# A masked attention layer and its routing, moved from their own stages into the slot timetable of the self-attention

## What is computed

```
x = x + _L1_attn_ref(_layernorm(x), ...)                  # 16 heads, rope, 100 keys
x = x + _L1_xattn_ref(_layernorm(x), ctx, ctx, mask, ...) # 16 heads, 361 keys
x = x + _L1_ffn_ref(_layernorm(x), ...)                   # top 1 of 8 experts
```

```
scores = jnp.where(attn_mask[:, None, :, :], -jnp.inf, scores)
A = jax.nn.softmax(scores, axis=-1)
...
gate_logits = jnp.einsum('bsd,ed->bse', x, gate_w) + gate_b + expert_bias
top_idx = jnp.argmax(gate_logits, axis=-1)
```

## Time and profile before

| | us |
|---|---|
| median of 3 runs | 1853.81 (1851.31 to 1858.56) |
| profiled execution, its own time | 1856.58 |
| span of that execution | 1854.9 |
| PE busy in it | 1511.9 (82%) |
| DVE, ACT, POOL busy | 835.1, 668.0, 460.0 |
| mean granted clock of PE | 0.909 |

### The profile page before, as it was taken

One profiled execution on the slowest core, in us unless ns is written; L12 is line 12 of the kernel. 1 busy time (PEld: TensorE's weight loads), 2 busy tenths in 40 slices (PEclk: granted clock), 3 DMA queues, 4 the chain that ended last, 5 costly groups with the idle time before them and its releaser, 6 DMA issues. The chain is left out here.

```text
span 1854.9 us, 31750 instructions
## 1 busy us (share of the span) xinstructions
PE 1511.9 (82%) x11682; PEld 1136.9 (61%) x11682; DVE 835.1 (45%) x2354; ACT 668.0 (36%) x1339; POOL 460.0 (25%) x426
## 2 busy tenths in 40 slices
PE   4988994588888899999999938988499999419992
PEld 2555652266655566888888825655266666319991
DVE  4666445467666442122222145665367776421111
ACT  1443341456544411222222224556355555102230
POOL 1212010001223353566666410111011110130003
PEclk9999997699988899999999967999599999659996
DMA  6432333777765223777777535553777774219994
GB/s 241 135 114 81 106 112 98 160 133 128 119 103 96 57 55 87 206 192 195 204 191 199 121 86 109 108 125 95 123 134 133 132 130 83 97 54 356 342 343 123
DMA packets 262658, 264.60 MB, mean 143 GB/s; under 512 B 118012, under 2 KB 235988, under 8 KB 256916
## 3 DMA queue, kind: packets, MB, share of 16 engines
q1 hardware_dynamic: 218516, 232.01, 48.7%
q0 software_dynamic: 41152, 28.50, 8.2%
q10 hardware_dynamic: 2880, 2.62, 0.4%
HBM read 202.35 MB, written 60.48 MB: 142 GB/s over the span
## 5 line engine op out<-in xcount | busy, mean ns | idle before, releaser
L2675 PE MATMUL cross_ps_score<-cross_q,cross_k 128*128 128x250 f32 x1024 | 223.4, 376 | 0.8 <-DVE cross_q L3090 0.8
L2675 PEld LDWEIGHTS cross_ps_score<-cross_q,cross_k 128*128 128x128 f32 x1024 | 195.5, 191 | 23.8 <-DVE cross_q L3090 1.0
L3099 DVE TENSOR_TENSOR cross_prob<-cross_act_,cross_ps_score 128x250 f32<-128x250 f32 x128 | 53.2, 416 | 268.2 <-ACT cross_act_ L2795 268.2
L3178 POOL DMA_INDIRECT x_sum<-cross_ye,cross_token x64 | 128.6, 2009 | 80.7 <-ACT cross_ye L2801 68.6
L1454 DVE CUSTOM_DVE_ANT_0 attn_masked_score<-attn_ps_score,attn_mask 100x361 bf16<-100x361 f32 x256 | 123.6, 532 | 54.2 <-PE attn_ps_score L1272 46.1
L1424 ACT ACTIVATE attn_prob<-attn_ps_prob 128x400 f32<-128x400 f32 (+1 forms) x192 | 94.7, 503 | 116.0 <-PE attn_ps_prob L1314 115.1
L2822 DVE TENSOR_REDUCE cross_nmax<-cross_ps_score 100x2 f32<-100x722 f32 x128 | 112.0, 904 | 50.5 <-PE cross_ps_score L2442 46.3
L2705 ACT ACTIVATE cross_prob<-cross_ps_prob 128x400 f32<-128x400 f32 (+1 forms) x192 | 94.7, 505 | 78.5 <-PE cross_ps_prob L2476 69.1
L2687 PE MATMUL cross_ps_prob<-cross_val,cross_prob 128*125 128x256 f32 x512 | 115.8, 379 | 0.0
L2795 ACT ACTIVATE cross_act_<-cross_ps_score 128x250 f32<-128x250 f32 x128 | 48.5, 379 | 167.7 <-PE cross_ps_score L2675 167.7
L2687 PEld LDWEIGHTS cross_ps_prob<-cross_val,cross_prob 128*125 128x125 f32 x512 | 93.5, 188 | 12.8
(11 more groups left out here) (383 smaller groups left out, 2900.4 us busy)
## 6 DMA issues: line engine op xcount, KB each, us to landing
experts_w<-in_w SPq DMA_DIRECT2D x40, 1024.0 KB, 7.4
k_stack<-mixer_part SPq DMA_DIRECT2D x32, 541.5 KB, 3.6
cross_k<-in_wg SPq DMA_DIRECT2D x32, 512.0 KB
cross_k<-in_wu SPq DMA_DIRECT2D x32, 512.0 KB
cross_val<-in_wd SPq DMA_DIRECT2D x32, 512.0 KB
cross_k<-k_stack SPq DMA_DIRECT2D x32, 270.8 KB
attn_k<-k_stack SPq DMA_DIRECT2D x32, 270.8 KB
mixer_ctx<-in_ctx_t POOLq DMA_DIRECT2D x16, 361.0 KB, 4.5
```

The costliest lines, as they stand in the source:

```text
L2675: ins = nc.tensor.matmul(ps_pre[m][:, side, 0:CAP], w[s][:, k, m * P:(m + 1) * P], xt[s][:, k, :], start=(k == 0), stop=(k == KD - 1))
L3178: g.indirect_dma_start(prog.x_sum, bass.IndirectOffsetOnAxis(token[:, 2 * e + t:2 * e + t + 1], 0), ye[s][:, t, :], None, compute_op=ALU.a ...
```

## The change

`stage_self`, `stage_attention` and `stage_route1` are gone; `stage_layer1` does the work of all three up to the scatters. Its first part is the timetable of `stage_self` with the same slots. In the change:

- The slots go on for the masked layer, 12 for a sequence, written out for all 16 sequences with no hardware loop. Its head, that is the loads, the score units and the values of sequence 0, stands at slots 64 to 75, where the self-attention finishes its sequence 15 (slots 64 to 67) and the last four sequences' queries are made (slots 71 to 78).
- The rows stay in `prog.x2`; the stores and loads of rows between the stages are gone, also in `stage_combine1`. The normalised rows of the routing are kept in `prog.kept`.
- Key tiles `m_k` lie in the memory of the self-attention's query and key stacks, context tiles in that of `xt`, so that their first loads wait for the last units of sequence 15. The queries `m_q` have tiles of their own.
- The maxima of both halves go through one transpose (slot 10), behind all 8 score units, in place of two. ACT, no longer DVE, copies the values and the turned rows out of PSUM. The value bias is put through the output projection once and is part of `m_bias_sum`.
- For each sequence b of the masked layer the routing's steps run two sequences behind: moments and root at slots 7 and 8 of the period in which its projection is done, `normalise5` at 10, `turn5` at 11 on PE, the copy of the turned rows (`xt5`) on ACT at slot 0 and `gate_logits` on PE at slot 1 of the next period, `gate_biased` on DVE at slot 2. `m_to_rows`, at slot 3, waits for it, since both write `ps_misc`. The top expert is found for a group of four sequences at once, at slots 4, 6, 8 and 9. The counting follows after the last slot, as before.
- Masks have three buffers. The first two are loaded on SP's queue right behind the four loads of x, the zeroing DMA of `expert_in` (2.6 MB) behind them, and POOL turns the two masks ahead of its first root.

```diff
@@ -275,6 +275,8 @@
         self.up2 = nc.alloc_sbuf_tensor("up2", [P, NUP, GT], F32)
         at = START["w_mlp1"][0]
         self.x2 = self.packed[0:T, at:at + B * D].rearrange("t (b d) -> t b d", b=B)
+        at = START["x0_wq"][0]
+        self.kept = self.packed[0:T, at:at + B * D].rearrange("t (b d) -> t b d", b=B)
         at = START["chunk_keep"][0]
         self.act2 = self.packed[:, at:at + NUP * GT].rearrange("p (u t) -> p u t", u=NUP)
 
-def stage_attention(prog, layer):
...
-def stage_self(prog):
+def stage_layer1(prog):
...
-    SLOTS = range(STATS_AT, GROUP * (NG - 1) + STORE_4_AT + 1)
...
+    M_UNITS = NQ * NKT
+    M_FROM = NQ * B + M_UNITS
...
+    M_SCORE_AT = {0: 0, 1: 1, 2: 2, 4: 3, 5: 4, 6: 5, 7: 6, 8: 7}
...
+    M_SHIFT_B, M_LAST_AV, M_LOGITS, M_BIASED, M_ROWS, M_TURN, M_OUT = 0, 1, 1, 2, 3, 5, 7
...
+    SLOTS = range(STATS_AT, M_FROM + M_UNITS * (B + 2))
...
+    def masked_slot(slot):
+
+        return divmod(slot - M_FROM, M_UNITS) if slot >= M_FROM - M_UNITS else (None, None)
...
-                def store_x(m):
-                    sp.wait_ge(v_out, G * (m + 1))
-                    sp.dma_start(group_rows(prog.x[4], m), prog.x2[:, m * G:(m + 1) * G]).then_inc(x_stored, 16)
+                def load_half(b, h):
+                    s = b % 2
+                    if h == 0:
+                        sp.wait_ge(stored[2], KD * len(Q_PARTS) * 16 * (b // G + 1))
...
                 for m in range(NG):
                     sp.dma_start(prog.x2[:, m * G:(m + 1) * G], group_rows(prog.x[3], m)).then_inc(x_in[m], 16)
+                for b in range(2):
+                    load_mask(b)
+                sp.wait_ge(zero_set, 1)
+                sp.dma_start(prog.expert_in.rearrange("(p n) d -> p n d", p=P),
+                             zeros[:].unsqueeze(1).broadcast_to([P, TILES1 * E1_ROWS // P, D])).then_inc(zeroed, 16)
...
-                        store_x(group_at(slot, STORE_4_AT))
                         store_parts("q4", group_at(slot, STORE_4_AT))
-                sp.wait_ge(stored[2], NG * KD * len(Q_PARTS) * 16)
-                sp.wait_ge(x_stored, NG * 16)
+                    if slot == M_FROM - M_UNITS:
+                        sp.wait_ge(pe_prob, NQ * B)
+                        for h in range(2):
+                            load_half(0, h)
+                        sp.wait_ge(pe_val, B)
+                        load_src(0)
+                        for h in range(2):
+                            load_half(1, h)
+                        load_src(1)
+                    b, k = masked_slot(slot)
+                    if in_range(b) and b + 2 < B:
+                        if k == 0:
+                            load_mask(b + 2)
+                            sp.wait_ge(m_pe_val, NKT * (b + 1))
+                            load_src(b + 2)
+                        if k == M_UNITS // 2:
+                            sp.wait_ge(m_pe_prob, M_UNITS * b + M_UNITS // 2)
+                            load_half(b + 2, 0)
+                        if k == M_UNITS - 1:
+                            sp.wait_ge(m_pe_prob, M_UNITS * (b + 1))
+                            load_half(b + 2, 1)
 
...
+                def m_to_rows(b):
+                    pe.wait_ge(m_acc, b + 1)
+                    if b == 0:
+                        pe.wait_ge(m_bias, 1)
+                    if b > 0:
+                        pe.wait_ge(v_gate_bias, b)
...
+                def turn5(b):
+                    pe.wait_ge(v_norm5, b + 1)
+                    for k in range(KD):
+                        ins = nc.tensor.transpose(ps_misc[:, k * T:(k + 1) * T], prog.kept[:, b, k * P:(k + 1) * P],
+                                                  ident[0:T, 0:T])
+                    ins.then_inc(pe_turn5, 1)
+
+                def gate_logits(b):
+                    pe.wait_ge(a_xt5, b + 1)
+                    for k in range(KD):
+                        ins = nc.tensor.matmul(ps_misc[0:T, LOGIT_COLS:LOGIT_COLS + E1], xt5[:, k, :],
+                                               prog.w("f1_gate_w", KD)[:, k, :], start=(k == 0), stop=(k == KD - 1))
...
+                    b, k = masked_slot(slot)
+                    if in_range(b):
+                        m_prob_unit(b, k)
+                    if b is None:
+                        continue
+                    if in_range(b - 1) and k == M_LAST_AV:
+                        m_weigh_values(b - 1, NQ - 1)
+                    if in_range(b - 2) and k == M_LOGITS:
+                        gate_logits(b - 2)
+                    if in_range(b) and k in M_AV_AT:
+                        m_weigh_values(b, M_AV_AT[k])
+                    if in_range(b - 1):
+                        if k == M_ROWS:
+                            m_to_rows(b - 1)
+                        if k == M_TURN:
+                            m_turn_rows(b - 1)
+                        if k == M_OUT:
+                            m_project(b - 1)
+                    if in_range(b + 1):
+                        if k in M_SCORE_AT:
+                            m_score_unit(b + 1, M_SCORE_AT[k])
+                        if k == M_SHIFT:
+                            m_shift_rows(b + 1)
+                        if k == M_VALUES:
+                            m_values(b + 1)
+                    if in_range(b - 1) and k == M_TURN5:
+                        turn5(b - 1)
...
+                        m_exp(b, k)
+                        if k == M_SHIFT_B:
+                            m_shift_half(b, 1)
+                            m_values(b, NKT - 1)
+                    if in_range(b - 2) and k == M_SHIFT_B:
+                        turn5(b - 2)
+                    if in_range(b - 1):
+                        if k == M_LAST_AV:
+                            m_keep_acc(b - 1)
+                        if k == M_TURN:
+                            m_turn_rows(b - 1)
+                    if b == -1 and k in (0, 6):
+                        m_select_heads(k // 6)
+                    if in_range(b + 1):
+                        if k == M_SHIFT:
+                            m_shift_half(b + 1, 0)
+                        if k == M_VALUES:
+                            for t in range(NKT - 1):
+                                m_values(b + 1, t)
...
+                def m_project(b):
+                    ve.wait_ge(m_base, b + 1)
+                    ve.wait_ge(m_pe_out, b + 1)
+                    nc.vector.tensor_tensor(prog.x2[:, b, :], ps_misc[0:T, 0:D], base[b % 2][:], ALU.add).then_inc(m_out, 1)
+                    ve.wait_ge(m_out, b + 1)
+                    nc.vector.bn_stats(stats4[:, b % 2, :], prog.x2[:, b, :]).then_inc(v_stats5, 1)
+
...
+                    if in_range(b - 2) and k == M_BIASED:
+                        gate_biased(b - 2)
+                    if in_range(b - 1):
+                        if k == M_ROWS:
+                            m_to_rows(b - 1)
+                        if k == M_OUT:
+                            m_project(b - 1)
+                    if in_range(b + 1) and k in M_SCORE_AT:
+                        m_score_unit(b + 1, M_SCORE_AT[k])
+                        if M_SCORE_AT[k] == M_NU - 1:
+                            m_split_shift(b + 1)
+                    if in_range(b - 1):
+                        if k == M_MEAN:
+                            means5(b - 1)
+                        if k == M_NORMAL:
+                            normalise5(b - 1)
+                    if in_range(b - 2) and (b - 2) % G == G - 1 and k in M_ROUTE_AT:
+                        route((b - 2) // G, M_ROUTE_AT.index(k))
+                ve.wait_ge(v_hot, NG)
...
+                    if slot == STATS_AT:
+                        set_mask(0)
+                        set_mask(1)
+                    b, k = masked_slot(slot)
+                    if b is None:
+                        continue
+                    if k == 0 and in_range(b):
+                        m_set_base(b)
+                    if k == 0 and b >= 0 and in_range(b + 2):
+                        set_mask(b + 2)
+                    if k == M_MEAN and in_range(b - 1):
+                        root5(b - 1)
+                g.wait_ge(zeroed, 16)
...
-def stage_route1(prog):
...
-                    ve.wait_ge(x_in[k], 16)
                     ve.wait_ge(got_in[k], 16 * G)
-                    nc.vector.tensor_tensor(acc[:, here], got[:, here], acc[:, here], ALU.add).then_inc(v_out, 1)
+                    nc.vector.tensor_tensor(acc[:, here], got[:, here], prog.x2[:, here], ALU.add).then_inc(v_out, 1)
...
-    stage_self(prog)
-    stage_attention(prog, 2)
-    stage_route1(prog)
+    stage_layer1(prog)
```

More of the change, by code:

```diff
@@ L3607, in _ @@
             def _(sp):
-                for k in range(NG):
-                    here = slice(k * G, (k + 1) * G)
-                    sp.dma_start(acc[:, here], prog.x[5][here].rearrange("g t d -> t g d")).then_inc(x_in[k], 16)
                 for k in range(NG):
```

1048 lines of the change are left out of this document (397 added, 651 removed).

## The result

The changed kernel takes 1823.18 us (median of 4 runs, 1821.55 to 1826.27), the kernel before 1852.56 in the same set; the ratio is 0.9837, 95% interval 0.9817 to 0.9857. The prediction was 1831 in a range of 1804 to 1855, faster. The profiled execution took 1824.3 us, 32.3 less than the one of before.

The account below looks back on a forecast made before the run. PE, nearly saturated in the masked attention, was taken as the bound, with two seams to fill. Terms -5.5 + 19.0 - 29.5 - 2.0 + 40.8 gave +22.8 gained: 1833.8 us profiled, 1831 median, range 1804 to 1855.

Parts of the forecast that it names:

- the two seams: Self-attention to masked attention, 49.5 us, and last masked output to last top expert, 47 us; the change fills both.
- B: Seam from self-attention's last unit to the end of the first masked values: 30.5 instead of 49.5 us, +19.0.
- E: Routing from last masked output to last top expert: 6.1 us instead of 46.95, +40.8.
- A: Start of the block: first root later because masks' loads and turning precede it, -5.5 us, bounds -7 and -1.
- C: Fifteen masked periods: a full period of 17.57 us, bounds 16.5 and 18.3; -29.5 in all.
- three waits: New PE waits per masked period: turned rows' copy +0.9, gate bias +0.55, all score units before the maxima's transpose +1.05.
- The cross-check of 17.5 from layer 0: Masked period estimated from layer 0's cross attention, 15.45 us a period, plus 12 mask matmuls of 0.17: 17.5.
- D: Last sequence, end of values to output: 18.4 us instead of 16.4, from two new waits and the turn, -2.0.
- The bound of 57: Claim that the change is worth it so long as the masked periods' cost stays under 57 us or so.
- R1: Rival: added slots cost nothing, PE keeps 15.5 us a masked period; 1805 us; chance 0.18.
- R2: Rival: waits make PE's clock fall in the masked periods, 20.0 us each; 1862 us; chance 0.12.
- R3: Rival: the seam between self-attention and masked attention isn't filled, gaining only +5; 1845 us; chance 0.08.

Follow-up runs that it names:

- masks-late runs: Changed kernel with the first two masks loaded and turned late: 1818.63 us, ratio 0.9802; with only their turning late, on another chip: 1794.00 us, ratio 0.9780.
- late turning alone: Changed kernel with the first two masks loaded as before but turned by POOL only at slot 44: 1794.00 us on another chip, ratio 0.9780.
- the gate elsewhere: Changed kernel with gate_logits and gate_biased moved from slots 1 and 2 to slot 9, top experts found at slot 11: 1812.24 us, ratio 0.9763.
- late routing: Changed kernel with turning, gate logits, biases and top expert of all 16 sequences behind the last slot: 1836.88 us, ratio 0.9904.
- The last kernel: Changed kernel with gate_logits at slot 9, maxima's transpose inside the values, their copies behind value copies, masks late, first-half loads early: 1786.29 us, ratio 0.9664.
- the run with more waits: Changed kernel with eight unneeded ACT copies ahead of the copy of the turned rows, on another chip: 1840.14 us, ratio 1.0049.

## Why the prediction was right, and where it wasn't

**What bounds it.** That the two seams are filled and the full stage pays was right in all terms' signs. B and E, 61 us together, came within 1.5 of their sizes. For E (6.1 for 5.84) that was a row of steps with lengths from the trace. In B the first masked score was placed well (11.3 behind the last unit, measured 11.0), but the rest is partly luck: from there to the start of the values it took 15.5 where 13.6 was reckoned, and the values took 2.8, as in a steady period, where 5.4 was taken over from before.

**A** was right in place and nearly in size (-6.25 for -5.5), and the masks-late runs show the cause: POOL's order, not the DMA queue. The masks landed at 1088.7, not at 1085; I had taken their landing from the end of x's traffic, though a load's landing behind its own issue (issued until 1082.83, landed 5.8 later) was the nearer measure. The order that I drew from the Trainium skill (DMA: Bandwidth & Descriptors, "Queues, rings and completion order": each DMA engine takes its descriptors in ring order), the masks behind x, is borne out as far as the trace goes, with the first moments from 1082.77 on and the masks at 1088.67. That the mask loads cost x nothing is shown by the runs: taking them away left the root where late turning alone put it, 6.77 and 6.72 behind the issue.

**C** is the term that was mis-sized: -21.8 for -29.5, the period 16.96 for 17.57. All three waits stood where I put them, at 0.74, 0.23 and 0.83 instead of 0.90, 0.55 and 1.05, in sum 1.80 for 2.50. The rest of the period, 15.16 for 15.07, looks right but is so by luck. Two terms of the base were read wrong: 15.30 is the stage divided by 15, shortened by its first values being long (5.42 for 2.82), while the steady period is 15.48; and the wait of 0.23 that I took off stands only before the first values. In a steady period of before (1460.20 to 1475.72) PE is busy for 14.88 of 15.52 and the only wait that shows is the 0.52. With both put right the same table gives 17.98, and it is then the added work that was reckoned too high as well, +0.52 where the rest grew by about 0.2. Why the waits came out shorter I can only guess: the hand table counted each handover at its full length on an engine that was just then free. The cross-check of 17.5 from layer 0 was off the same way and so was no support. The waits turned out not to be independent: one covered another of 0.51 (the runs with the gate elsewhere and with late routing), and both had one cause, ACT's copy of the second half.

**D** was mis-sized too (-0.5 for -2.0). I added the first two new waits and took none away; yet the last sequence of before had its own wait for the copy of the maxima (0.83 at 1574.42), which is gone. The first new wait was 1.05 in it (at 1582.00).

**The bound of 57** for C in the prediction doesn't follow from its terms: -5.5 + 19.0 - 2.0 + 40.8 is 52.3.

**R1**, slots that cost nothing, didn't come: the period went from 15.48 to 16.96. The last kernel shows that it was within reach, and that what spoke for it, the idle time of DVE and ACT, was real.

**R2** didn't come in the change, but it was rightly a rival. The Trainium skill describes such a swing for short idle stretches between groups of matmuls (TensorE: Matmul & The Clock Gate, "A second HAM failure mode: psum-queue depth-cycling"; the section that the prediction names stands just ahead of it and is on long waits for transfers). The windows of the run with more waits agree with it, 1.00 and 0.91 by turns, and those of the change, at 1.00 with waits of their own, don't. The run shows that 1.6 us more of wait a period, made in one piece by more work on ACT, was enough for it; the break-even period of 19.3 that I gave was near, at 19.56 the kernel is 0.5% slower than before.

**R3** didn't come; the seam gained 20.2. It spoke of the first half's loads being late; in the run with the first half's loads early it is the second half's that are (2.60 of wait).

The profile gained 32.3 where 22.8 was forecast: C makes 7.7 of the 9.5 between them, D 1.5, B 1.2, E 0.3, A -0.75, and the unchanged stages -0.5.

## What to carry to other kernels

When work of a finished stage moves into a saturated one, its busy time can be the small part of the price (here PE is busy 15.17 us a period for 14.88 of before), and the waits in the engines' lists the large one (1.80 for about 0.6). Not all of them came from the work that moved in: 0.83, and 0.52 that stood hidden behind the 0.74, are there without the routing too and belong to the single transpose and to the copies that ACT took over. Here each could be moved to a slot where the producer was done. Look for a copy that stands in front of others though its input is old, and for a wait that stands in front of work that doesn't need it. An operation that waits for a transfer and stands first in an engine's list holds everything behind it.

## What the runs showed that I had not expected

With waits of 0.74, 0.23 and 0.83 in 16.96 us the granted clock is 1.00 in every steady period. With 2.32 in place of the 0.74, and more work on ACT, it is 0.91 in ten periods of thirteen and 1.00 in three, every third or fourth, though the wait is the same in all of them. An average over the stage (0.94) hides that. And by the profile PE was busy for 100.00 of 100 us over six sequences of a masked attention with softmax and routing.
